# Half of one attention unit in twelve transposed through DRAM and VectorE instead of TensorE

## What is computed

```python
hn = group_norm(x, gn1_scale, gn1_bias)
qkv = einsum('bchw,oc->bohw', hn, w_qkv) + b_qkv         # 8 heads of 64 channels
wgt = softmax(einsum('bct,bcs->bts', q*scale, k*scale), -1)   # 1024 x 1024 for each head
a = einsum('bts,bcs->bct', wgt, v)
x = x + group_norm(einsum('bchw,oc->bohw', a, w_proj) + b_proj)
```

## Time and profile before

| | |
|---|---|
| median of three runs | 3375.3 us (3374.86 to 3377.05) |
| the profiled execution, its own time | 3375.88 us |
| its span, first to last instruction | 3373.7 us |
| TensorE matmul busy | 3351.2 us (99%) |
| VectorE busy | 2132.7 us (63%) |
| ScalarE busy | 1838.7 us (55%) |
| GpSimd busy | 1064.3 us (32%) |
| granted TensorE clock | 1.000 on average |

### The profile page before, as it was taken

How to read it: one execution, slowest core, us unless ns; L and a number is a source line. 1 busy time by engine, 2 the same in 40 slices (tenths; PEclk the granted TensorE clock), 3 DMA queues, 4 the chain that set the end, 5 groups by cost and what they waited for, 6 DMA issues and landing times.

```text
span 3373.7 us, 51950 instructions
## 1 busy us (share of the span) xinstructions
PE 3351.2 (99%) x16816; PEld 2777.5 (82%) x16816; DVE 2132.7 (63%) x3489; ACT 1838.7 (55%) x3094; POOL 1064.3 (32%) x947
## 2 busy tenths in 40 slices
PE   8999999999999999999999999999999999999999
PEld 6888888888888888888888888888888888888887
DVE  5677357773578745786457854578555784557844
ACT  4677227862378523784337842388333882347822
POOL 1344104441045410453104531145211452124511
PEclk9999999999999999999999999999999999999999
DMA  8522244313534125331253212442224422343212
GB/s 340 149 67 59 79 131 124 93 34 94 140 99 101 62 57 151 103 86 76 53 167 91 73 75 76 144 101 63 93 61 144 98 63 94 92 139 70 63 57 75
DMA packets 109871, 332.15 MB, mean 98 GB/s; under 512 B 21760, under 2 KB 54784, under 8 KB 98816
## 3 DMA queue, kind: packets, MB, share of 16 engines
q1 hardware_dynamic: 107648, 322.15, 33.3%
q10 hardware_dynamic: 1920, 6.29, 0.9%
HBM read 162.68 MB, written 31.49 MB: 58 GB/s over the span
## 4 chain that ended last, share of the span: by engine, by line
PE 94%; DMA 2%; issue 1%; DVE 1%; SPq 1%; ACT 1%; POOL 0%; POOLq 0%; DVEq 0%
PE big L514 25%; PE big L648 14%; PE ops L634 14%; PE tps L619 14%; PE big L746 7%; PE big L655 5%; PE tps L819 5%; PE ops L819 5%; PE ops L598 3%; DMA ST<-ST 2%; PE tps L746 1%; SPq L419 0%; PE ops L746 0%; SPq L484 0%; PE ops L788 0%
## 5 line engine op out<-in xcount | busy, mean ns | idle before, releaser
L1097 POOL TENSOR_SCALAR PB<-PB,small 128x1024 f32<-128x1024 f32 x576 | 648.7, 1127 | 1294.8 <-DVE small L1342 1277.2
L1347 DVE TENSOR_TENSOR PT<-tps,PT 128x512 fp32r<-128x512 f32 x1024 | 652.5, 679 | 42.1 <-ACT PT L954 41.7
L1336 DVE TENSOR_REDUCE small<-big 128x1 f32<-128x1024 f32 x512 | 625.2, 1221 | 85.1 <-PE big L648 81.8
L954 ACT ACTIVATE PT<-tps 128x512 fp32r<-128x512 f32 x1024 | 564.1, 597 | 158.3 <-PE tps L619 155.4
L948 ACT ACTIVATE PB<-big,small 128x1024 f32<-128x1024 f32 x512 | 572.8, 1119 | 94.8 <-DVE small L1336 91.8
L634 PE MATMUL ops<-PT,VT 128*128 128x512 f32 x2048 | 599.1, 414 | 0.0
L648 PE MATMUL big<-ST 128*128 128x512 f32 x2048 | 554.2, 392 | 3.5 <-DMA ST<-ST 3.5
L619 PEld LDWEIGHTS tps<-ident,PB 128*128 128x128 f32 x4096 | 470.2, 140 | 95.4 <-DVE PT L1347 30.9
L619 PE MATMUL tps<-ident,PB 128*128 128x128 f32 x4096 | 545.7, 274 | 0.9
L648 PEld LDWEIGHTS big<-ST 128*128 128x128 f32 x2048 | 382.6, 188 | 91.5 <-issue 6.1
L634 PEld LDWEIGHTS ops<-PT,VT 128*128 128x128 f32 x2048 | 346.1, 189 | 47.1 <-DVE PT L1347 5.0
(11 more groups left out here) (188 smaller groups left out, 4911.7 us busy)
## 6 DMA issues: line engine op xcount, KB each, us to landing
ST<-ST SPq DMA_DIRECT2D x360, 256.0 KB, 5.3
W<-d_qk SPq DMA_DIRECT2D x32, 1024.0 KB, 7.0
W<-PB SPq DMA_DIRECT2D x256, 128.0 KB, 2.4
X<-in_x SPq DMA_DIRECT2D x8, 2048.0 KB, 10.2
W<-d_wp SPq DMA_DIRECT2D x8, 2048.0 KB, 11.9
W<-d_g SPq DMA_DIRECT2D x8, 2048.0 KB, 11.8
W<-d_m SPq DMA_DIRECT2D x8, 2048.0 KB, 7.7
W<-d_u SPq DMA_DIRECT2D x8, 2048.0 KB, 13.2
```

The costliest lines, as they stand in the source:

```text
L954: act_fn(pt_slot(u, s)[:, 0, :], tps[n % 2][:], ACT.Copy).then_inc(s_pt_hi, 1)
L1097: nc.gpsimd.tensor_scalar(PB[:, i, :], PB[:, i, :], rinv[:, i:i + 1], 1.0, ALU.mult, ALU.mult)\
L1336: V.tensor_reduce(negmax[:, i:i + 1], tile(("s", 4 * u + tb))[:], axis=AX.X, op=ALU.max, negate=True).then_inc(s_row_max, 1)
L1347: V.tensor_tensor(pt_slot(u, s)[:, 1, :], tps[n % 2][:], pt_slot(u, s)[:, 0, :].bitcast(f32), ALU.subtract).then_inc(s_pt_ready, 1)
```

## The change

In each batch the first units of pairs 0, 1 and 2 (units 0, 4 and 8) no longer have slots 4 to 7 transposed by TensorE. Instead SyncE stores the second half of the keys of the four normalised rows to DRAM (four DMAs of 256 KB, each once its row is normalised), waits for that, and loads the four quarters of it back into `F0`, a part of `X`, with eight DMAs of 128 KB in runs of 512 bytes, so that a 128 by 128 block lies with quarters of rows and columns exchanged. VectorE then turns each slot in 32 by 32 blocks (`square`), ScalarE rounds it from SBUF (`moved_hi`), VectorE makes the rest (`moved_lo`). `X` is loaded from DRAM later, and scaled in steps 50 to 56 instead of 20 to 29.

So that a quarter is contiguous, the keys of the second half of these pairs are stored in another order when the key tile is split: the column of key 128 s + 32 q + r is 128 q + 4 r + s. All four units of such a pair see that order. Units 1 to 3 of the pair are still transposed by TensorE, now with a stationary operand whose columns stand four elements (16 bytes) apart; VectorE's turn reads with the same step, and the split of the key half writes with it.

The query-key tiles are made keys first, second half first, and in steps 5, 7, 8 and 10 of a pair instead of 5, 7, 9 and 11. The values of the moved slots wait: TensorE's steps 7 and 8 have one slot of values each, step 9 two, step 10 four.

```diff
-QK_STEPS = (5, 7, 9, 11)
+QK_STEPS = (5, 7, 8, 10)
+MOVED = [4 * pair for pair in range(PAIRS - 1)]
+MOVED_SLOTS = [8 * u + s for u in MOVED for s in range(4, NT)]
+def transposed(step):
+    n = 2 * (step - LAG)
+    return [m for m in (n, n + 1) if m >= 0 and m not in MOVED_SLOTS]
+def valued(step):
+    n = 2 * (step - LAG) - 2
+    return [m for m in (n, n + 1) if m >= 0 and m not in MOVED_SLOTS and m + 1 not in MOVED_SLOTS[::4]]
+SQUARES_FIRST, SQUARES_LAST = {7: (4, 5)}, {9: (6, 7)}
+MOVED_LO = {7: (4, 5), 9: (6, 7)}
+MOVED_VALUES = {8: (3,), 9: (4, 5), 10: (6, 7)}
-X_SCALE_STEPS = (20, 23, 26, 29)
+X_SCALE_STEPS = (50, 52, 54, 56)
...
+        def keys_by_turn(pair, half, row):
+            if half and 4 * pair in MOVED:
+                return row.rearrange("p (q r s) -> p s q r", q=QUARTERS, s=4)
+            return row.rearrange("p (s q r) -> p s q r", q=QUARTERS, s=4)
...
+            def move_quarters(b, u):
+                if u:
+                    sp.wait_ge(s_squared, squared_count(b, 8 * (u - 4) + NT - 1))
+                    own_wait(sp)
+                for t in range(KB):
+                    sp.wait_ge(s_p_norm, b * 72 + 4 * u + t + 1)
+                    own_wait(sp)
+                    sp.dma_start(d_e[t], PB[:, t, HALF:N]).then_inc(s_moved_out[t // 2], 16)
+                for part in range(2):
+                    sp.wait_ge(s_moved_out[part], (b * len(MOVED) + MOVED.index(u) + 1) * 32)
+                    own_wait(sp)
+                    for q in range(QUARTERS):
+                        sp.dma_start(F0[32 * q:32 * q + 32, 2 * part:2 * part + 2, :],
+                                     d_e[2 * part:2 * part + 2].rearrange("t (q p) n -> p (t q) n", p=32)
+                                     [:, :, P * q:P * q + P]).then_inc(s_moved, 16)
...
-                sp.dma_start(X[:], src_x(b)).then_inc(s_x_res, 16)
+                move_quarters(b, 0)
...
+                move_quarters(b, 4)
                 stack_head(b, 2, 0)
                 stack_head(b, 2, 1)
+                move_quarters(b, 8)
                 stack_head(b, 3, 0)
+                sp.wait_ge(s_pt_ready, b * 144 + MOVED_SLOTS[-1] + 1)
+                own_wait(sp)
+                sp.dma_start(X[:], src_x(b)).then_inc(s_x_res, 16)
...
                     for t in range(4):
-                        last = nc.tensor.transpose(tps[n % 2][:, P * t:P * t + P],
-                                                   PB[:, 4 * (u % 2) + t, P * s:P * s + P], ident[:])
+                        row = PB[:, 4 * (u % 2) + t, :]
+                        if s >= 4 and u // 4 * 4 in MOVED:
+                            keys = row[:, HALF:N].rearrange("p (k s) -> p s k", s=4)[:, s - 4, :]
+                        else:
+                            keys = row[:, P * s:P * s + P]
+                        last = nc.tensor.transpose(tps[n % 2][:, P * t:P * t + P], keys, ident[:])
...
+                def moved_hi(n):
+                    act.wait_ge(s_squared, squared_count(b, n))
+                    act.wait_ge(s_values_read, b * len(MOVED_SLOTS) + MOVED_SLOTS.index(n) + 1)
+                    act_fn(pt_slot(n // 8, n % 8)[:, 0, :], squared(n % 8), ACT.Copy).then_inc(s_moved_hi, 1)
...
+                def square(n):
+                    u, s = n // 8, n % 8
+                    if s == 4:
+                        dve.wait_ge(s_moved, (b * len(MOVED) + MOVED.index(u) + 1) * 32 * QUARTERS)
+                    V.transpose(squared(s).rearrange("p (t q r) -> p t q r", t=KB, q=QUARTERS),
+                                F0.rearrange("p t (q r s) -> p s t q r", q=QUARTERS, s=4)[:, s - 4, :, :, :])\
+                     .then_inc(s_squared, 1)
...
                 for step in range(STEPS0 + LAG):
+                    for m in of_moved(step, SQUARES_FIRST):
+                        square(m)
                     if qk_part(step) is not None:
                         qk_lo(qk_part(step))
...
+                    for m in of_moved(step, SQUARES_LAST):
+                        square(m)
+                    for m in of_moved(step, MOVED_LO):
+                        moved_lo(m)
+                    for m in transposed(step):
+                        pt_lo(m // 8, m % 8)
```

More of the change, by code:

```diff
@@ L46, in qk_part, with of_moved @@
     return None
+MOVED = [4 * pair for pair in range(PAIRS - 1)]
+MOVED_SLOTS = [8 * u + s for u in MOVED for s in range(4, NT)]
+def of_moved(step, table):
+    unit = 4 * (step // 16)
+    return [8 * unit + s for s in table.get(step % 16, ())] if unit in MOVED else []
+def transposed(step):
[7 more added lines that the diff above has]
+MOVED_VALUES = {8: (3,), 9: (4, 5), 10: (6, 7)}
 def a_parts(step):
@@ L233, in build @@
         s_ld_u = sem("ld_u")
+        s_moved_out = [sem(f"moved_out{i}") for i in range(2)]
+        s_moved = sem("moved")
+        s_squared = sem("squared")
+        s_moved_hi = sem("moved_hi")
+        s_values_read = sem("values_read")
         s_stack_a = sem("stack_a")
@@ L603, in project_qk @@
                 def project_qk(j):
-                    pair, what, half = j // 4, j % 4 // 2, j % 2
+                    pair, what, half = j // 4, 1 - j % 4 // 2, 1 - j % 2
                     if j % 4 == 0:
@@ L694, in body @@
                         out_block(proj0, 0, 1, 0)
[L695 to L700, removed]
+                    for m in of_moved(step, MOVED_VALUES):
+                        values0(m)
+                    for m in transposed(step):
+                        transposes(m // 8, m % 8)
+                    for m in valued(step):
+                        values0(m)
                 values0(8 * UNITS0 - 2)
@@ L947, in exps @@
                     i = 4 * (u % 2) + tb
+                    if u - 2 in MOVED and tb == 0:
+                        for part in range(2):
+                            act.wait_ge(s_moved_out[part], (b * len(MOVED) + MOVED.index(u - 2) + 1) * 32)
                     act_fn(PB[:, i, :], t[:], ACT.Exp, bias=negmax[:, i:i + 1], accum_out=rowsum[:, i:i + 1])\
@@ L990, in body @@
                         qk_hi(qk_part(step))
[L991 to L994, removed]
+                    for m in of_moved(step, SQUARES_FIRST):
+                        moved_hi(m)
+                    for m in transposed(step):
+                        pt_hi(m // 8, m % 8)
+                    if tb == 2 and u >= 2 and u - 2 not in MOVED:
+                        corr(u - 2, 0)
+                    if tb == 3 and u - 2 in MOVED:
                         corr(u - 2, 0)
```

50 lines of the change are left out of this document (37 added, 13 removed).

## The result

The changed kernel took 3393.42 us (median of 6 runs, 3391.47 to 3395.35), the kernel before 3375.76 beside it: a ratio of 1.0052, 95% interval 1.0041 to 1.0063. It is 17.7 us slower, where 35 us faster was forecast. The profiled execution took 3393.87 us, with a span of 3392.1.

What follows compares the result with a forecast made beforehand. TensorE, 99% busy and 94% of the chain, was taken as the bound. Moved stretch: 20.0 us work plus 0.55 waits, 1.45 less than before, times 24 is 35; 3375.9 - 35 = 3341 us, range 3330 to 3475.

Steps and rivals of the forecast that it cites:

- an instruction that leaves TensorE is worth its own pace: TensorE's chain: 384 transposes removed, 1.74 us in each of 24 units, take 41.8 us off the path.
- The layout of steps 7 to 12: Hand-made order of work and waits after the change: the stretch falls from 21.99 to 20.5 us, 1.45 less.
- 0.55 us a unit: Waits added to 20.0 us of TensorE work in the moved stretch, single ones about 0.1 to 0.3 us.
- The split of the first key tile: Step 5: if VectorE's strided part doubled, pt_lo and two transposes late by some 0.5 us, 16 times, 8 us.
- the likeliest case: Whole kernel with all covers holding, chance 0.54: from 3330 to 3354 us.
- strided weight load taken at nothing: TensorE's 1152 transposes with a stationary operand stepping 16 bytes: no added time.
- The rival on the other side: The 1152 strided weight loads are slow: 126 us at twice the load, 3467; chance 0.30.
- The transfers come in time: Trip through DRAM before VectorE's turns: 7.6 us, in time by 1.7 and 3.3 us.
- The third rival: Steps 9 to 12: VectorE's missed waits cost 1.4 us more than laid out, nothing left, 3375; chance 0.07.

Runs made afterwards that it cites:

- staged kernel: The changed kernel with GpSimd writing the keys in the new order, so nothing reads or writes with a step of four: 3366.10 us, ratio 0.9973.
- old steps: The changed kernel with its query-key tiles in steps 5, 7, 9, 11 again: 3478.52 us, ratio 1.0306, +102.6 us against the kernel before.

## Why the prediction was wrong

**How the 17.7 us are made up.** From the table of stretches, times 8: the strided split of steps 5 and 6 +14.8, steps 7 to 12 -9.0, the rest +11.2, together +17.0. The rest holds 15 of the 18 groups of strided transposes that a batch has, at 0.08 to 0.10 us each about 1.4 us a batch, which is about its whole size. The forecast had -35 for steps 7 to 12 and nothing for the other two. From the runs: order -5.2; 384 transposes at their pace -41.8; what the way of a tile over ScalarE and VectorE keeps back even with nothing added, 31.4 - 15.6 = +15.8; turns, copies, transfers and GpSimd's split rows +21.5. That is -9.7, and it meets the staged kernel's -9.5 by construction, since the last term was taken from that kernel. The three strided terms are measured on their own: split +14.3, loads +10.6, turns of pair 0 +4.5. With them the sum is +19.7 against a measured +17.7. The terms come from different kernels, so that 2 us of the difference are open, and the size of one term depends on the others (the 102.6 us of the old steps shows how much).

**The step that failed: "an instruction that leaves TensorE is worth its own pace".** It was read from a share of 94%, which is a mean over all steps, and used in the two steps where it does not hold. The layout of steps 7 to 12 had the latency there as waits of 0.1 us. Removing transposes takes work out of just those steps in which TensorE must wait for a tile to pass ScalarE and VectorE: with nothing added at all, 288 transposes worth 31.4 us at their pace gave 7.5 in the old order and 15.6 in the new. The stretch of steps 7 to 12 came to 21.47 in pair 1, not 20.5, so 9 us were gained there in all and not 35.

**A wait of 0.1 us is not 0.1 us.** Waits were laid out at 0.55 us a unit. In the profile after, tile 8 and the scores of step 9 start 0.2 us late and then take 0.29 us more: 0.5 each, and the transposes of step 11 are 1.29 instead of 0.87, of which 0.08 is the strided load. That is 1.4 us a unit where 0.55 stood. More than half of the 0.29 is no slower work: the chain counts a group in an unbroken stream from the end of the one ahead, a late one from its own first matmul, and that adds the part of the modelled way through the array that would have lain under the group ahead (0.39 us for a matmul, 0.23 to the next, so 0.16). TensorE's timeline shows the rest: in tile 8 the second matmul starts 0.33 us behind the first (589.14, 589.47) instead of 0.23, so about 0.1 is a slower start.

**The split of the first key tile was mis-sized**: 8 us allowed outside the sum, 14.3 measured. Only VectorE's part was considered; ScalarE's write stands on the same way and lengthens by 0.5 us as well. The 8 us were in the range of the likeliest case, not in its sum.

**The strided weight load taken at nothing was 10.6 us.** The rival on the other side was right in its direction (the load itself is 60 to 70 ns longer) and twelve times too large, since the pace takes up only 0.010 us a load. The rule in the Trainium skill, "SBUF — State Buffer", section "Door 1: The DMA port swizzle", that fewer than two hits on a 16-byte line lose rate, agrees with each of the four strided instructions here; it does not give what the pace of an engine makes of it. In the Trainium skill, "Vector Engine (DVE) Microarchitecture Reference", section 5.2, a source that hops 4 KiB at every element takes 1.73 ns a column instead of 1.05, 1.65 times as long. Here the step is 16 bytes: the split's 1.16 us against 0.75 is 1.55 times, the turn's 1080 ns against 693 is 1.56 times.

**What held.** The transfers come in time (no idle ahead of L1458; store 2.0, loads 2.9 us, the loads' issue 3.8 for eight). The turns are off the chain in pairs 1 and 2, though 1.08 us each; in pair 0 their extra length costs 4.5 us in all. `moved_hi` is 632 ns. VectorE's total work is not what binds (-1.2 us for short turns); its place in the fixed order is. The third rival, that the stretch eats the gain by waits which the layout missed, was given 0.07 and is the nearest to what happened, though not where it looked: of the 1.4 us a unit, 0.5 is at tile 8, 0.5 at the scores of step 9, both behind `qk_lo`, and only the rest in step 11, where the longest wait was forecast. It also ended at "nothing is left", and the strided terms made the kernel slower than that. That the measured time lies within the stated 3330 to 3475 is no merit: the upper end was there for a doubled weight load, which did not happen.

## What to carry to other kernels

Before pricing an instruction that leaves the busiest engine, take it out of the chain of its own steps and see what ends the next wait: where a tile must pass two other engines before the next can start, work that is removed turns into waiting. Price the latency of each instruction on that way, a strided write above all, apart from its share of busy time, and count a near miss of TensorE at about 0.3 us more than the wait that the chain shows. To test such a change cheaply, take the work out and add nothing: that run gives the gain before any cost, in its own order of work.

## What the runs showed of the hardware

- When TensorE just misses a semaphore, the group behind it is 0.29 us longer in the chain (a tile 3.03 instead of 2.74, scores 1.20 instead of 0.91), in the changed and in the staged kernel; about 0.1 of it is a slower start, the rest the modelled way through the array.
- Single fp32 elements 16 bytes apart, 512 columns: ScalarE's write 0.69 to 1.19 us, VectorE's split 0.75 to 1.16, its 32x32 turn 693 to 1080 ns. TensorE's weight load of 128 columns goes from 138 to between 197 and 212 ns, and the pace of transposes from 0.109 to 0.119 us.
- Behind a stand of 2.12 us TensorE's granted clock was 0.55 for 3.6 us, in a kernel that is 98% busy; it fell so behind 22 of 24 such stands, and behind 8 of 24 stands of 2.15 us in another kernel.
